# Squares of the input weights computed on ScalarE instead of VectorE, in front of the first correction row

## The chip, the cores and the metric

The kernel runs on the 8 cores of one Trainium2 chip. Each core computes 2048 of the 16384 tokens with the same program; no core waits for another. The metric is the device time in microseconds (us) of the slowest core. The engines of a core are named as in the profile: PE (TensorE, matmuls), PEld (its weight loads), DVE (VectorE), ACT (ScalarE), POOL (GpSimd) and SP (SyncE); POOL and SP issue the DMAs here.

## The reference

Positive random features replace attention, then a gated feed-forward layer; both with a residual and a layer norm.

```
def _rfs(xw, ab, AB, gs):
    dot_products = einsum('...d,rd->...r', xw, ab[:, None] * gs)
    correction = (0.5 * sum(xw * xw, axis=-1))[..., None] * (ab * ab)
    return 1.0 / sqrt(NUM_RFS) * AB * exp(dot_products - correction)

ab = xis;  AB = exp(xis)
weights = _rfs(input_weights, ab, AB, proj_matrix)     # [1024, 1024]
feats   = _rfs(x, ab, AB, proj_matrix)                 # [16384, 1024]
x = layernorm(x + einsum('bsr,or->bso', feats, weights))
gate = x @ (w_gate/127).T;  up = x @ (w_up/127).T      # 1024 -> 3072
x = layernorm(x + (silu(gate) * up) @ (w_down/127).T)  # 3072 -> 1024
```

What the change touches is `sum(xw * xw)` for `xw = input_weights`: the squares of a 1024 x 1024 matrix, summed over its inner dimension.

## The kernel before

A core's tokens are worked in four tiles of 512. In the first half (features), tile by tile, `emit_mm1(t)` computes the projections of the tile on PE in eight groups (`rc`) of eight 128x512 matmuls (line 268) and one single-row matmul (line 273) that adds the correction; ACT turns each group into features by an exponential (line 281). `emit_mm2(t)` multiplies the features with `weights` (lines 410, 416 and 422) and layer norm follows. The second half is the feed-forward layer (lines 565, 603, 658 to 674).

The order on every engine is the order in which the program is written: `Sched` keeps one list for each engine, `wait` puts a wait for a semaphore's value into it, and `inc` an instruction that raises one. ACT and DVE also wait for their own instruction before, through their own semaphore. No scheduler moves anything, so what stands behind a wait in a list waits too.

The start goes as follows.

- POOL issues all loads one behind the other (line 169): `xfm` of tile 0, the row `xisr`, two halves of `projT`, then `iwT` (the input weights, 8192 columns on 128 partitions), `xfm` of tile 1 and later `wgT`. `iwT` has a semaphore of its own, `Liw`.
- `emit_xsq(0)`: DVE squares tile 0 of x into the buffer XSQ (line 200). `emit_ones_mm(0)`: PE sums the squares with a column of ones (line 235, tile `pt3`). `emit_srow(0)`: ACT scales the sum and writes the row that the correction matmuls read (line 249).
- `emit_mm1(0)` waits for that row, with `em.wait("tensor", "SE", ev["se_srow", t])`, and runs its eight groups.
- `emit_iwsq(dk)`, for dk 0 to 7: DVE squares one eighth of `iwT` (128x1024, line 213) into one of two halves of XSQ. `emit_swones(dk)`: PE sums it with two 1x512 matmuls (line 289), accumulating over dk in PSUM. DVE waits before square dk for the sums of dk - 2, since the halves alternate.
- `emit_swrow()`: ACT makes the correction row of the weights (line 301). `emit_dotw()`: PE projects the input weights, eight groups of sixteen 128x512 matmuls (line 313) and two single-row ones (line 320), and ACT writes `weights` by an exponential (line 332).
- `emit_xsq(1)`: DVE squares tile 1 of x into XSQ, once the last sum of the weights' squares has been read from it.

X1TB is a buffer of 8192 columns that is first written by the evacuation of transposed layer-norm outputs in tile 1 (line 456), and by an SP load of `x1s` into its second half behind that.

Of the kernel before, what the change touches and what calls it, by code (L numbers as in the profile page):

```python
# [14 lines left out]
AF = mybir.ActivationFunctionType  # L15
OP = mybir.AluOpType
# [7 lines left out]
DK = D // 128  # L24
# [11 lines left out]
X1TB_O = X1TOK_O + 4096  # L36
PROJT_O = X1TB_O + 8192
IWT_O = PROJT_O + 8192
WT_O = IWT_O + 8192
XFM_O = WT_O + 8192  # L40
XSQ_O = XFM_O + 8192
# [52 lines left out]
def build_nc(stage=3, lnlv=5):  # L94
# [13 lines left out]
    with ExitStack() as stack:  # L108
        e = stack.enter_context
# [13 lines left out]
        em = Sched(sems)  # L123
        ev = {}

        def bf(a, b):
            return BF[:, a:a + b]

        def bfr(a, b):
            return BF[0:1, a:a + b]  # L130
# [8 lines left out]
        ones_col = bf(ONES_O, 1)  # L139
# [31 lines left out]
        def xfsem(t):  # L171
            return "Lxf" + str(t % 2)
# [20 lines left out]
        def emit_xsq(t):  # L193
            em.wait("vector", xfsem(t), ev["ld_xfm", t])
            if t >= 1:
                em.wait("vector", "MM", ev.get(("mm_swones", DK - 1)) if t == 1 else ev["mm_ones", t - 1])
            for h in range(2):
                ev["gs_xsq", t, h] = em.inc(
                    "vector", "VE",
                    lambda e, t=t, h=h: e.tensor_tensor(  # L200
                        bf(XSQ_O + h * 2048, 2048),
                        bf(XFM_O + (t % 2) * 4096 + h * 2048, 2048),
                        bf(XFM_O + (t % 2) * 4096 + h * 2048, 2048), OP.mult))

        def emit_iwsq(dk):
            em.wait("vector", "Liw", ev["ld_iwT"])
            if dk == 0:
                em.wait("vector", "MM", ev["mm_ones", 0])
            if dk >= 2:
                em.wait("vector", "MM", ev["mm_swones", dk - 2])  # L210
            ev["gs_iwsq", dk] = em.inc(
                "vector", "VE",
                lambda e, dk=dk: e.tensor_tensor(  # L213
                    bf(XSQ_O + (dk % 2) * 1024, 1024), bf(IWT_O + dk * 1024, 1024),
                    bf(IWT_O + dk * 1024, 1024), OP.mult))

        ftmp = fa(FTMP_O, DK)
        em.wait("vector", "XR", XR_ALL)
# [8 lines left out]
        def emit_ones_mm(t):  # L227
            em.wait("tensor", "VE", ev["ve_consts"])
            if t >= 1:
                em.wait("tensor", "SE", ev["se_srow", t - 1])  # L230
            for dk in range(DK):
                if dk % 4 == 0:
                    em.wait("tensor", "VE", ev["gs_xsq", t, dk // 4])
                def f(e, dk=dk, t=t):
                    return e.matmul(prow[:, :], ones_col,  # L235
                                    bf(XSQ_O + dk * 512, 512),
                                    start=(dk == 0), stop=(dk == DK - 1))
                if dk == DK - 1:
                    ev["mm_ones", t] = em.inc("tensor", "MM", f)
                else:  # L240
                    em.raw("tensor", lambda e, f=f: f(e))

        def emit_srow(t):
            em.wait("scalar", "MM", ev["mm_ones", t])
            if t >= 2:
                em.wait("scalar", "MM", ev["mm_dot", 8 * (t - 2) + RC - 1])
            ev["se_srow", t] = em.inc(
                "scalar", "SE",
                lambda e, t=t: e.activation(  # L249
                    bfr(SROW_O + (t % 2) * 512, 512), prow[:, :], AF.Identity,  # L250
                    bias=c512[0:1, :], scale=-0.5))
# [31 lines left out]
                        bias=biasF[:, rc:rc + 1], scale=xisc[:, rc:rc + 1]))  # L283

        def emit_swones(dk):
            em.wait("tensor", "VE", ev["gs_iwsq", dk])
            for oh in range(2):
                def f(e, dk=dk, oh=oh):
                    return e.matmul(P1[0:1, 1024 + oh * 512:1024 + oh * 512 + 512],
                                    ones_col, bf(XSQ_O + (dk % 2) * 1024 + oh * 512, 512),  # L290
                                    start=(dk == 0), stop=(dk == DK - 1))
                if oh == 1:
                    ev["mm_swones", dk] = em.inc("tensor", "MM", f)
                else:
                    em.raw("tensor", lambda e, f=f: f(e))
# [139 lines left out]
        def emit_tr(t, m):  # L435
            i = 4 * t + m
            em.wait("tensor", "SE", ev["se_apply", i])
            if i >= 1:
                em.wait("tensor", "VE", ev["ve_evac", i - 1])
            for dk in range(DK):  # L440
                def f(e, dk=dk, i=i):
                    return e.transpose(ptr[:, dk * 128:dk * 128 + 128],  # L442
                                       bf(X1TOK_O + (i % 4) * 1024 + dk * 128, 128),
                                       ident)
                if dk == DK - 1:
                    ev["mm_tr", i] = em.inc("tensor", "MM", f)
                else:
                    em.raw("tensor", lambda e, f=f: f(e))
            em.wait("vector", "MM", ev["mm_tr", i])
            if m == 0:  # L450
                em.wait("vector", "XSS", 16 * t)
            dst = BF[:, X1TB_O:X1TB_O + 4096].rearrange(
                "p (dk t) -> p dk t", dk=DK)[:, :, m * 128:m * 128 + 128]
            srcp = ptr[:, :].rearrange("p (dk t) -> p dk t", dk=DK)
            ev["ve_evac", i] = em.inc(
                "vector", "VE", lambda e, dst=dst, srcp=srcp: e.tensor_copy(dst, srcp))
            if m == 3:
                em.wait("sync", "VE", ev["ve_evac", i])
                em.wait("sync", "XSS", 16 * t)
                ev["xs_st", t] = em.inc(  # L460
                    "sync", "XSS",
                    lambda e, t=t: e.dma_start(
                        x1s_h[:, t * 4096:(t + 1) * 4096], bf(X1TB_O, 4096)), 16)
                if t == 0:
                    em.wait("sync", "XSS", ev["xs_st", 0])
                    ev["xs_ld", 0] = em.inc(
                        "sync", "XSL",
                        lambda e: e.dma_start(bf(X1TB_O + 4096, 4096),
                                              x1s_h[:, 0:4096]), 16)

        emit_xsq(0)
        emit_ones_mm(0)
        emit_srow(0)
        emit_mm1(0)
        for dk in range(DK):
            emit_iwsq(dk)
            emit_swones(dk)
        emit_swrow()
        emit_dotw()
        ev["ld_wgT"] = dma("gpsimd", "Lwg", bf(WGT_O, 24576), wgT_h[:, :])  # L480
        emit_xsq(1)
        emit_ones_mm(1)
        emit_srow(1)
# [136 lines left out]
        for pi, t in enumerate(B_ORDER):  # L620
# [26 lines left out]
            for m in range(4):  # L647
                i = 4 * pi + m
# [72 lines left out]
def _get_nc():  # L721
    global _NC_CACHE
    if _NC_CACHE is None:
        _NC_CACHE = build_nc()
    return _NC_CACHE
# [42 lines left out]
```

How the kernel before makes its waits and increments, by code:

```python
    def wait(self, eng, sem, val):  # L74
        if val is None or val <= 0:
            return
        assert val <= self.c[sem], f"wait on future event {sem}={val} > {self.c[sem]}"
        key = (eng, sem)
        if self.lastwait.get(key, 0) >= val:
            return
        self.lastwait[key] = val
        h = self.sems[sem]
        self.q[eng].append(lambda e, h=h, v=val: e.wait_ge(h, v))
# [1 line left out]
    def inc(self, eng, sem, fn, n=1):  # L85
        if (eng in ("vector", "scalar")) or (eng == "gpsimd" and sem == "GS"):
            self.wait(eng, sem, self.c[sem])
        h = self.sems[sem]
        self.c[sem] += n
        self.q[eng].append(lambda e, fn=fn, h=h, n=n: fn(e).then_inc(h, n))
        return self.c[sem]
# [2 lines left out]
def build_nc(stage=3, lnlv=5):  # L94
# [56 lines left out]
            if hc < 8:  # L151
                base = XSQ_O + hc * 512
            elif hc < 16:
                base = FEATS_O + (hc - 8) * 512
            elif hc < 20:
                base = IWT_O + 6144 + (hc - 16) * 512
            else:
                base = X1TOK_O + (hc - 20) * 512
            return bf(base + lo, n)
        em.raw("sync", lambda e: e.dma_start(fa(FXISC_O, DK), xisc_h[:, :]).then_inc(sems["XR"], 16))
        em.c["XR"] += 16
        XR_ALL = em.c["XR"]
```

## Time and profile before

| | us |
|---|---|
| median of 3 runs | 738.04 |
| lowest and highest of them | 737.9, 738.67 |
| the profiled execution's own time | 738.42 |
| its span on the slowest core (core 1) | 736.9 |
| spans of the eight cores | 733.8 to 736.9 |
| PE busy on core 1 | 702.6 (95% of the span) |
| DVE busy, ACT busy | 182.6, 197.0 |

All rows come from one profiled execution, and where nothing else is said, from core 1. Times count from the first instruction of that core. A timeline row merges instructions of one line that follow each other (xcount), gives the start and the length in us, and in brackets how long the engine had been idle before and what released it. The clock (PEclk) is the share of full TensorE speed that the chip granted.

### The profile page before, as it was taken

What the parts mean: (1) busy time and instruction counts of PE and PEld (TensorE: products, weight loads), DVE (VectorE), ACT (ScalarE), POOL (GpSimd) and SP (SyncE); (2) the same over time, 40 slices, a digit from 0 to 9 for tenths busy, and PEclk for the clock granted to TensorE, in tenths of its full rate; (3) what the DMA queues carried; (4) which work ended last, traced back from release to release, by engine and by line L of the source; (5) the groups of instructions that cost most, each with busy time, mean ns of one, the idle gap of its engine ahead of it and who ended that gap; (6) DMA issues with size and microseconds to landing.
All of it is one profiled execution on the core that took longest, in us unless ns stands there. A gap on an engine that the chain in (4) does not pass through costs nothing.

```text
span 736.9 us, 9045 instructions; the slowest of 8 cores (733.8 to 736.9 us)
## 1 busy us (share of the span) xinstructions
PE 702.6 (95%) x3424; PEld 314.2 (43%) x3424; DVE 182.6 (25%) x327; ACT 197.0 (27%) x322; POOL 8.0 (1%) x19
## 2 busy tenths in 40 slices
PE   1989999999979999999999999999999999999994
PEld 0323444444444444444444444444444444444442
DVE  1040143444352111122221121221212131211222
ACT  0312235353551111043311105231110523111122
POOL 2000000000000000000000000000000000000000
PEclk9999999999989999999999999999999999999997
DMA  8990030591057000001200000120000100000011
GB/s 124 167 367 28 1 58 1 121 390 60 1 225 289 1 1 1 1 28 58 87 0 1 1 1 29 58 86 0 1 0 3 57 29 29 0 1 2 1 58 57
DMA packets 5547, 44.63 MB, mean 61 GB/s; under 512 B 768, under 2 KB 768, under 8 KB 2816
## 3 DMA queue, kind: packets, MB, share of 16 engines
q0 software_dynamic: 1904, 27.27, 13.4%
q1 hardware_dynamic: 3600, 16.78, 6.1%
q8 instruction: 28, 0.46, 0.3%
q14 instruction: 15, 0.12, 0.1%
HBM read 30.42 MB, written 12.58 MB: 58 GB/s over the span
## 4 chain that ended last, share of the span: by engine, by line
PE 90%; DMA 5%; DVE 2%; ACT 1%; issue 1%; POOL 0%; DVEq 0%; ACTq 0%; POOLq 0%
PE pt L603 23%; PE P L565 22%; PE P L658 22%; PE P L410 6%; PE P L268 6%; DMA bfarena<-iwT 5%; PE P L313 4%; PE P L273 1%; PE P L664 1%; PE P L674 1%; PE P L416 1%; PE P L422 1%; PE pt L442 1%; PE pt L235 1%; DVE bfarena L213 1%
## 5 line engine op out<-in xcount | busy, mean ns | idle before, releaser
L565 PE MATMUL P<-bfarena 128*128 128x512 bf16 x768 | 184.6, 382 | 0.4 <-ACT bfarena L584 0.4
L603 PE MATMUL pt<-bfarena 128*128 128x512 bf16 x768 | 181.8, 379 | 0.0
L658 PE MATMUL P<-bfarena 128*128 128x512 bf16 x736 | 163.2, 379 | 0.0
L616 DVE SCALAR_TENSOR_TENSOR bfarena<-pt,bfarena 128x512 bf16<-128x512 f32 x96 | 66.4, 692 | 245.5 <-PE pt L603 236.8
L584 ACT ACTIVATE bfarena<-P 128x512 bf16<-128x512 f32 x96 | 57.3, 597 | 237.2 <-PE P L565 229.1
L565 PEld LDWEIGHTS P<-bfarena 128*128 128x128 bf16 x768 | 75.1, 98 | 93.2 <-issue 2.5
L603 PEld LDWEIGHTS pt<-bfarena 128*128 128x128 bf16 x768 | 74.9, 97 | 92.5
L658 PEld LDWEIGHTS P<-bfarena 128*128 128x128 bf16 x736 | 71.9, 98 | 88.7
L357 DVE TENSOR_SCALAR_CACHE_REDUCE bfarena<-P 128x1024 bf16<-128x1024 f32 x32 | 39.2, 1225 | 202.6 <-PE P L674 144.9
L268 PE MATMUL P<-bfarena 128*128 128x512 bf16 x256 | 62.9, 388 | 2.3 <-ACT bfarena L249 2.3
L377 ACT ACTIVATE f32arena<-f32arena 128x1 f32<-128x1 f32 x32 | 9.4, 295 | 176.5 <-DVE f32arena L374 175.6
L410 PE MATMUL P<-bfarena 128*128 128x512 bf16 x224 | 51.5, 379 | 0.0
L281 ACT ACTIVATE bfarena<-P,f32arena 128x512 bf16<-128x512 f32 x32 | 24.9, 778 | 57.1 <-PE P L273 57.1
L268 PEld LDWEIGHTS P<-bfarena 128*128 128x128 bf16 x256 | 23.0, 99 | 34.3 <-issue 11.2
L313 PE MATMUL P<-bfarena 128*128 128x512 bf16 x128 | 31.0, 396 | 1.4 <-ACT bfarena L301 1.4
L410 PEld LDWEIGHTS P<-bfarena 128*128 128x128 bf16 x224 | 21.3, 98 | 24.3 <-issue 0.4
L235 PE MATMUL pt<-bfarena 128*1 128x512 bf16 x32 | 9.4, 440 | 13.6 <-DVE bfarena L200 13.5
L313 PEld LDWEIGHTS P<-bfarena 128*128 128x128 bf16 x128 | 12.3, 101 | 19.6 <-issue 7.1
L388 ACT ACTIVATE bfarena<-bfarena,f32arena 128x1024 bf16<-128x1024 bf16 x16 | 19.8, 1240 | 1.5
L388 ACT ACTIVATE f32arena<-bfarena,f32arena 128x1024 f32<-128x1024 bf16 x16 | 19.8, 1240 | 1.5
L367 DVE SCALAR_TENSOR_TENSOR f32arena<-bfarena 128x1024 f32<-128x1024 bf16 x16 | 19.6, 1225 | 2.0 <-DVE f32arena L359 0.5
L367 DVE SCALAR_TENSOR_TENSOR bfarena<-bfarena 128x1024 bf16<-128x1024 bf16 x16 | 19.6, 1225 | 1.7
(53 smaller groups left out, 225.3 us busy)
## 6 DMA issues: line engine op xcount, KB each, us to landing
out<-f32arena SPq DMA_DIRECT2D x16, 512.0 KB, 2.6
bfarena<-wgT POOLq DMA_DIRECT2D x1, 6144.0 KB, 54.2
bfarena<-wdT POOLq DMA_DIRECT2D x3, 2048.0 KB, 14.5
bfarena<-wuT POOLq DMA_DIRECT2D x1, 4608.0 KB, 26.9
bfarena<-xfm POOLq DMA_DIRECT2D x4, 1024.0 KB, 12.6
x1s<-bfarena SPq DMA_DIRECT2D x4, 1024.0 KB, 4.8
bfarena<-x1s SPq DMA_DIRECT2D x4, 1024.0 KB, 7.2
bfarena<-projT POOLq DMA_DIRECT2D x2, 1024.0 KB, 19.5
```

The lines of the kernel that those rows point to most:

```text
L268: em.raw("tensor", lambda e, rc=rc, dk=dk, xb=xb, ps=pslice: e.matmul(ps, pjap(rc, dk), bf(xb + dk * 512, 512), start=(dk == 0), stop=False))
L281: lambda e, rc=rc, ps=pslice: e.activation(bf(FEATS_O + rc * 512, 512), ps, AF.Exp, bias=biasF[:, rc:rc + 1], scale=xisc[:, rc:rc + 1]))
L313: em.raw("tensor", lambda e, rc=rc, dk=dk, oh=oh, base=base: e.matmul(P1[:, base + oh * 512:base + oh * 512 + 512], pjap(rc, dk), bf(IWT_O ...
L357: e.tensor_scalar(dv, ps, 1.0, 0.0, OP.mult, OP.add, accum_out=negS))
L367: e.scalar_tensor_tensor(out_ap, dv, 1.0, dv, OP.mult, OP.mult, accum_out=s2))
L388: lambda e, dv=dv, out_ap=out_ap, rc_=rc_, nmrs=nmrs: e.activation(out_ap, dv, AF.Identity, scale=rc_[:, 0:1], bias=nmrs))
L410: em.raw("tensor", lambda e, rc=rc, oh=oh, m=m, base=base: e.matmul(P1[:, base + oh * 512:base + oh * 512 + 512], bf(FEATS_O + rc * 512 + ...
L565: return e.matmul(pg, bf(WGT_O + dk * 3072 + hc * 128, 128), bf(xb1 + dk * 512, 512), start=(dk == 0), stop=(dk == DK - 1))
L584: "scalar", "SE", lambda e, j=j, pg=pg: e.activation(sg_ap(j), pg, AF.Silu, scale=1.0 / 127.0))
L603: return e.matmul(puj, bf(wu_off + hc * 128, 128), bf(xb1 + dk * 512, 512), start=(dk == 0), stop=(dk == DK - 1))
L616: "vector", "VE", lambda e, j=j, hc=hc, puj=puj: e.scalar_tensor_tensor(hact_ap(hc, 0, 512), puj, 1.0 / 16129.0, sg_ap(j), OP.mult, OP.mult))
L658: e.matmul(P1[:, base + oh * 512:base + oh * 512 + 512], hact_ap(hc, m * 128, 128), bf(reg + (hc % 8) * 1024 + oh * 512, 512), start=(hc = ...
```

## The change

The squares of the input weights go from DVE (`tensor_tensor` with OP.mult, into the two halves of XSQ) to ACT (`activation` with AF.Square, into the eight eighths of X1TB, one for each dk). ACT's squares wait for `Liw`, as DVE's did. In the written order six of them stand between `emit_ones_mm(0)` and `emit_srow(0)`, two behind `emit_srow(0)`, and all of them ahead of `emit_mm1(0)`. The sums wait for ACT's semaphore instead of DVE's. Three waits on the last sum follow from the new buffer: DVE before the first evacuation into X1TB, SP before the load into its second half, while `emit_xsq(1)` now waits for `mm_ones, 0` alone.

```diff
         def emit_xsq(t):
             em.wait("vector", xfsem(t), ev["ld_xfm", t])
             if t >= 1:
-                em.wait("vector", "MM", ev.get(("mm_swones", DK - 1)) if t == 1 else ev["mm_ones", t - 1])
+                em.wait("vector", "MM", ev["mm_ones", t - 1])
...
         def emit_iwsq(dk):
-            em.wait("vector", "Liw", ev["ld_iwT"])
-            if dk == 0:
-                em.wait("vector", "MM", ev["mm_ones", 0])
-            if dk >= 2:
-                em.wait("vector", "MM", ev["mm_swones", dk - 2])
-            ev["gs_iwsq", dk] = em.inc(
-                "vector", "VE",
-                lambda e, dk=dk: e.tensor_tensor(
-                    bf(XSQ_O + (dk % 2) * 1024, 1024), bf(IWT_O + dk * 1024, 1024),
-                    bf(IWT_O + dk * 1024, 1024), OP.mult))
+            em.wait("scalar", "Liw", ev["ld_iwT"])
+            ev["se_iwsq", dk] = em.inc(
+                "scalar", "SE",
+                lambda e, dk=dk: e.activation(
+                    bf(X1TB_O + dk * 1024, 1024),
+                    bf(IWT_O + dk * 1024, 1024), AF.Square))
...
         def emit_swones(dk):
-            em.wait("tensor", "VE", ev["gs_iwsq", dk])
+            em.wait("tensor", "SE", ev["se_iwsq", dk])
             for oh in range(2):
                 def f(e, dk=dk, oh=oh):
                     return e.matmul(P1[0:1, 1024 + oh * 512:1024 + oh * 512 + 512],
-                                    ones_col, bf(XSQ_O + (dk % 2) * 1024 + oh * 512, 512),
+                                    ones_col,
+                                    bf(X1TB_O + dk * 1024 + oh * 512, 512),
                                     start=(dk == 0), stop=(dk == DK - 1))
...
             em.wait("vector", "MM", ev["mm_tr", i])
+            if i == 0:
+                em.wait("vector", "MM", ev["mm_swones", DK - 1])
...
                 if t == 0:
+                    em.wait("sync", "MM", ev["mm_swones", DK - 1])
                     em.wait("sync", "XSS", ev["xs_st", 0])
...
         emit_xsq(0)
         emit_ones_mm(0)
+        for dk in range(6):
+            emit_iwsq(dk)
         emit_srow(0)
+        emit_iwsq(6)
+        emit_iwsq(7)
         emit_mm1(0)
         for dk in range(DK):
-            emit_iwsq(dk)
             emit_swones(dk)
         emit_swrow()
         emit_dotw()
```

ACT's list at its start, before. Line 249 makes the correction row of tile 0, 281 the features, 301 the correction row of the weights; MM counts PE's instructions, SE ACT's own.

```order
L249 ACTIVATE bfarena<-pt,f32arena 1x512 [waits MM]
L281 ACTIVATE bfarena<-P,f32arena 128x512 [waits MM,SE] x8
L301 ACTIVATE bfarena<-P 1x1024 [waits MM,SE]
L332 ACTIVATE bfarena<-P,f32arena 128x1024 [waits MM,VE,SE]
L332 ACTIVATE bfarena<-P,f32arena 128x1024 [waits MM,SE] x7
L249 ACTIVATE bfarena<-pt,f32arena 1x512 [waits MM,SE]
```

And after, where line 209 is the new square and the lines 245, 277, 298 and 329 are those that were 249, 281, 301 and 332.

```order
L209 ACTIVATE bfarena<-bfarena 128x1024 [waits Liw]
L209 ACTIVATE bfarena<-bfarena 128x1024 [waits SE] x5
L245 ACTIVATE bfarena<-pt,f32arena 1x512 [waits MM,SE]
L209 ACTIVATE bfarena<-bfarena 128x1024 [waits SE] x2
L277 ACTIVATE bfarena<-P,f32arena 128x512 [waits MM,SE] x8
L298 ACTIVATE bfarena<-P 1x1024 [waits MM,SE]
L329 ACTIVATE bfarena<-P,f32arena 128x1024 [waits MM,VE,SE]
L329 ACTIVATE bfarena<-P,f32arena 128x1024 [waits MM,SE] x7
```

The instruction that waits for `Liw` is now the first of ACT's list, with the correction row of tile 0 behind it in seventh place.

PE's list at the end of `emit_mm1(0)`, before: the last group of the features, then the sums of the weights' squares (line 289), each pair with its wait for DVE (VE); five of the eight pairs are left out here.

```order
L268 MATMUL P<-bfarena 128x512 x7
L273 MATMUL P<-bfarena 128x512
L289 MATMUL P<-bfarena 1x512 [waits VE]
L289 MATMUL P<-bfarena 1x512
L289 MATMUL P<-bfarena 1x512 [waits VE]
L289 MATMUL P<-bfarena 1x512
L289 MATMUL P<-bfarena 1x512 [waits VE]
L289 MATMUL P<-bfarena 1x512
```

And after, where line 285 is the sum and line 310 the first matmul of `emit_dotw()`.

```order
L264 MATMUL P<-bfarena 128x512 x7
L269 MATMUL P<-bfarena 128x512
L285 MATMUL P<-bfarena 1x512 x16
L310 MATMUL P<-bfarena 128x512 [waits SE,Liw]
L310 MATMUL P<-bfarena 128x512 x15
```

The sixteen sums stand at the same place of PE's list, now with no wait among them. The wait for ACT's correction row ahead of `emit_mm1(0)` is where it was.

## Rows read from the trace of the kernel before

**Rows 1.** Spans and mean granted clock, three of the eight cores.

```profile
core 1: 736.9 us, clock 0.988
core 4: 736.5 us, clock 0.991
core 7: 735.3 us, clock 0.993
```

**Rows 2.** PE's waits, all of the span: total us, times, longest.

```profile
PE pt L235 <- DVE bfarena L200: 13.5, 1, 13.5
PE pt L442 <- DVE bfarena L456: 3.6, 2, 3.3
PE P L268 <- ACT bfarena L249: 2.3, 1, 2.3
PE P L289 <- DVE bfarena L213: 2.0, 8, 0.6
PE P L313 <- ACT bfarena L301: 1.4, 1, 1.4
```

**Rows 3.** Chain that ended last, in order of time, the load of iwT.

```profile
3.77 34.16 DMA bfarena<-iwT
```

**Rows 4.** Timeline of core 1, from the first ACT instruction to the first features.

```profile
17.20 1.28 ACT L249 ACT_TABLE_LOAD   x1 [17.20 <-PE pt L235]
18.50 0.68 ACT L249 ACTIVATE bfarena<-pt,f32arena 1x512 bf16<-1x512 f32 x1
...
19.43 3.52 PE L268 MATMUL P<-bfarena 128*128 128x512 bf16 x8 [2.31 <-ACT bfarena L249]
...
23.42 0.78 ACT L281 ACTIVATE bfarena<-P,f32arena 128x512 bf16<-128x512 f32 x1 [4.25 <-PE P L273]
...
25.59 0.78 ACT L281 ACTIVATE bfarena<-P,f32arena 128x512 bf16<-128x512 f32 x1 [1.39 <-PE P L273]
```

**Rows 5.** Timeline of core 1, from the end of emit_mm1(0) to emit_dotw().

```profile
38.05 0.39 PE L273 MATMUL P<-bfarena 1*128 1x512 bf16 x1
38.16 6.32 DVE L213 TENSOR_TENSOR bfarena<-bfarena 128x1024 bf16<-128x1024 bf16 x8 [23.43 <-DMA bfarena<-iwT]
...
39.00 0.59 PE L289 MATMUL P<-bfarena 128*1 128x512 bf16 x2 [0.56 <-DVE bfarena L213]
...
44.63 0.59 PE L289 MATMUL P<-bfarena 128*1 128x512 bf16 x2 [0.21 <-DVE bfarena L213]
45.37 1.01 ACT L301 ACTIVATE bfarena<-P 1x1024 bf16<-1x1024 f32 x1 [6.00 <-PE P L289]
...
46.64 5.31 PE L313 MATMUL P<-bfarena 128*128 128x512 bf16 x16 [1.42 <-ACT bfarena L301]
...
81.34 1.91 PE L235 MATMUL pt<-bfarena 128*1 128x512 bf16 x8
```

**Rows 6.** ACT's instructions grouped by line and form: count, busy us, mean ns.

```profile
L584 ACT ACTIVATE bfarena<-P 128x512 bf16<-128x512 f32 x96 | 57.3, 597 | 237.2 <-PE P L565 229.1 <-DVE bfarena L616 7.6
L281 ACT ACTIVATE bfarena<-P,f32arena 128x512 bf16<-128x512 f32 x32 | 24.9, 778 | 57.1 <-PE P L273 57.1
L388 ACT ACTIVATE bfarena<-bfarena,f32arena 128x1024 bf16<-128x1024 bf16 x16 | 19.8, 1240 | 1.5
L332 ACT ACTIVATE bfarena<-P,f32arena 128x1024 bf16<-128x1024 f32 x8 | 9.6, 1204 | 26.7 <-PE P L320 26.7
L301 ACT ACTIVATE bfarena<-P 1x1024 bf16<-1x1024 f32 x1 | 1.0, 1014 | 6.0 <-PE P L289 6.0
```

**Rows 7.** Timeline of core 1, two ACT instructions of a layer norm in a row.

```profile
91.81 0.30 ACT L384 ACTIVATE f32arena<-f32arena 128x1 f32<-128x1 f32 x1
92.19 1.24 ACT L388 ACTIVATE bfarena<-bfarena,f32arena 128x1024 bf16<-128x1024 bf16 x1
```

**Rows 8.** PE by stretch on core 1: us, busy (x), PEclk, DMA share, GB/s.

```profile
45.30:46.60 1.30, 0.00 (x0) 1.00 1.06 454
46.60:52.00 5.40, 5.36 (x17) 0.68 0.97 413
```

**Rows 9.** Timeline of core 4, the first group of emit_dotw().

```profile
46.35 3.65 PE L313 MATMUL P<-bfarena 128*128 128x512 bf16 x15 [1.42 <-ACT bfarena L301]
49.93 0.60 PE L320 MATMUL P<-bfarena 1*128 1x512 bf16 x2
```

**Rows 10.** Timeline of core 7, the correction row and the second group's features.

```profile
18.30 0.68 ACT L249 ACTIVATE bfarena<-pt,f32arena 1x512 bf16<-1x512 f32 x1
...
26.53 0.78 ACT L281 ACTIVATE bfarena<-P,f32arena 128x512 bf16<-128x512 f32 x1 [2.26 <-PE P L273]
```

## The prediction, made before the changed kernel had run

> **What bounds the kernel now.** I read four views, in this order. The cores first: core 1 ends last, core 4 0.4 us before it and core 7 1.6 us before it, and the program is the same on all, so one core's timeline can be followed as long as the spread is kept in mind [rows 1]. Then PE's waits, since PE is busy for 95% of the span. They are few: 13.5 us at the start for the first tile of x, 2.3 us for ACT's first correction row, 2.0 us in eight pieces for DVE's squares of the input weights, 1.4 us for the weights' correction row, and 3.6 us much later, for an evacuation [rows 2]. The edits touch the second, third and fourth. Third, the chain that ended last: it doesn't go through the features of tile 0 but through the load of iwT, issued at 3.77 and landing 34.16 us later, at 37.93 [rows 3]. So PE's work up to 38.4 lies beside a transfer, and nearly fills that time. Last, the timeline of the start, from which all terms come [rows 4, 5].
>
> In it the reader is to see two things. The features of tile 0 run from 19.43 to 38.44 and need nothing of iwT: what released them was the correction row on ACT, 18.50 to 19.18 [rows 4]. And DVE starts its squares at 38.16, 0.23 us behind the landing, while PE ends the features at 38.44: two things that end together [rows 5]. From 46.64 on PE runs almost without a pause, so a delay of that moment is a delay of the end.
>
> **The change part by part.** I follow core 1 to the start of the weights' projection (line 313), which is at 46.64 before. Nothing in the change touches the loads, so iwT still lands at 37.93.
>
> 1. *The wait for iwT moves ahead of the features.* ACT's list now begins with the square that waits for Liw. Behind it stand, on the same engine, five more squares and then the correction row of tile 0, and for that row waits all of PE's emit_mm1(0). DVE saw the landing 0.23 us later [rows 3, 5]; I give ACT the same, 38.16. Its first instruction carried the table load behind its wait: load at 17.20, 1.28 long, next instruction at 18.50 [rows 4]. So the first square starts at 38.16 + 1.30 = 39.46.
>
> 2. *Six squares.* The trace has no Square. The nearest is a 128x1024 SBUF to SBUF ACTIVATE with scale and bias read from memory, 1.240 us. Against the same from PSUM, 1.204, SBUF costs 0.036. The operands read from memory cost 0.18: 778 ns with them, 597 ns without, both 128x512. A 1x1024 one without them took 1.014. All of it in [rows 6]. So 1.240 - 0.18 = 1.06, or 1.014 + 0.036 = 1.05; I take 1.05, since the square reads no such operand, and keep 1.01 and 1.24 as bounds. Between two dependent ACT instructions lie 0.09 us (0.30 from 91.81 ends at 92.11, the next starts at 92.19) [rows 7]. Six squares: 5 x 1.14 + 1.05 = 6.75, ended at 46.21; bounds 6.5 and 7.9.
>
> 3. *The correction row and the features.* The row starts at 46.30, takes 0.68, ends at 46.98. PE came 0.25 later before (19.18 to 19.43) [rows 4], so the features start at 47.23 instead of 19.43: **27.80 us later**. They take the same 19.0 us. This includes their slow start: the first eight matmuls took 3.52 us where eight of the same length took 1.91 at full clock [rows 4, 5], which is the lower level, 1.2 GHz, after PE had idled. PE idles before this start in both kernels, for 2.3 us then and for about 30 now, and I take the same cost. Squares 6 and 7 take 2 x 1.14 = 2.3 us on ACT behind the row; the first features are due 4.25 us behind it [rows 4], so they are covered. Without that cover, if a square took over 2.1 us, the exponentials would come late.
>
> 4. *The sums lose their waits.* Before, the first sum started at 39.00, or 0.56 us of waiting behind the features, and the last ended at 45.22. After, all eight squares lie ready when the features end (near 66). Sixteen 1x512 matmuls at full clock: eight take 1.91 at line 235 [rows 5], so the distance is (1.91 - 0.38) / 7 = 0.22 and sixteen take 15 x 0.22 + 0.38 = 3.63. From 39.00 to 45.22 were 6.22: **2.6 us gained**, and **0.6 us** for the wait ahead of them. The bound on the other side is no gain, if the sums ran at the lower level: 16 x 0.44 = 7.0.
>
> 5. *The weights' correction row* keeps its 1.42 us of idle PE [rows 5]; it is what is late next when DVE's waits go.
>
> 6. *The clock of the weights' projection.* On core 1 the granted clock was 1.00 in 45.3 to 46.6 and 0.68 in the 5.4 us behind it (the lower level for most of a first group) [rows 8]: the first sixteen matmuls took 5.31. On core 4, behind the same 1.42 us of idle time, fifteen took 3.65 and the group's end came at 49.93 + 0.60, so 4.18 us after its start, against 5.85 us on core 1: the cost is 1.67 [rows 5, 8, 9]. Ahead of it PE had been fed in pairs with a pause each, on both. In the changed kernel it is fed without pauses, so I take the full clock on core 1, a gain of 1.67 there and of nothing on core 4. Both outcomes stay in the range.
>
> 7. *The rest costs nothing.* emit_xsq(1) no longer waits for the sums: off the path, since its reader stands behind the weights' projection. The two new waits for the last sum, on DVE before the first evacuation and on SP before the load into X1TB, ask for an event that is some 50 us old there (queued behind: the layer-norm work on DVE, stores of x1s on SP). DVE loses 8 squares, of which nothing waits.
>
> Two rules of the Trainium skill bear on this; nothing above depends on them. ScalarE: Activation LUTs, "Rules for kernel authors", gives multiplication to VectorE and not to ScalarE, which speaks against this change; the trace has DVE's eight squares in 6.32 us, 0.79 apiece with the gap, and by step 2 ACT's would be 1.14, so by that rule alone eight of them would cost 2.8 us more, off the path here once they lie ahead of the sums. The same page, "What ACT_TABLE_LOAD costs", adds a drain of about 1.38 us to a load of 1.283; the load agrees with [rows 4], but the next instruction there starts 0.02 us behind it, so the sum goes without the drain, and with it would be an estimated 1.4 us higher.
>
> **The sum.** Core 1: +27.80 - 0.60 - 2.6 = +24.6, less 1.67 for the clock, +22.9, to a span of 759.8. Core 4: 736.5 + 24.6 = 761.1, since iwT's landing drops out (both the old and the new start of the projection count from it) and it had nothing to regain. The slowest core then ends at 761.1, +24.2 against 736.9. I add 0.3 us for the slow start of the features, which was mostly hidden beside the load and is now on every core's path: from the start of the correction row to the second group's features core 1 took 25.59 - 18.50 = 7.09 us and core 7 26.53 - 18.30 = 8.23 [rows 4, 10], so the slowest of eight can pay up to 1.1 more. The profiled execution, 738.42 with a span of 736.9, would be at 762.9; the median of the runs, 738.04, is 0.4 lower and gives **762.5 us**.
>
> **The rivals.**
> - *One table doesn't serve all.* If the square's table lacks Identity and Exp, another load of 1.28 us comes ahead of the correction row, on the path; the further two, around squares 6 and 7, make 2 x 1.28 + 2.3 = 4.9 us on ACT against 4.25 to the first features, and those are not asked for by PE until its third group. So +1.3: 763.8. For it: no row shows Square. Against it: Identity and Exp run on one load at the start [rows 4]. (Trainium skill, ScalarE: Activation LUTs, "Table sets": cheap functions are in every set, though square isn't named there.) Chance 0.08.
> - *The clock turns against it.* The features' start like core 7's on the slowest core (+0.8 over my 0.3), and the lower level at the projection on a core that had not paid it before (core 4, +1.67): 762.5 + 2.5 = 765.0. For it: core 1's fall [rows 8]. Chance 0.08.
> - *Not slower: iwT comes early.* The new start of the projection is the landing plus 33.3 us (71.2 - 37.93), the old one 46.64. The change decides for itself if iwT lands by 13.3; then the squares run beside DVE's first ones and the gain of steps 4 and 6 is left, 738.0 - 3.2 - 1.3 = 733.5. Against it: 34.16 us from issue to landing, behind four loads that nothing here moves [rows 3]. Chance 0.02.
> - *The program doesn't hold back the row*, if ACT ran the correction row ahead of its squares. ACT's order is its list's; nothing speaks for it. The time would be about 735. Chance 0.01.
>
> **How the numbers follow.** The forecast has 0.81. Its own bounds: squares of 1.01 and 1.24 give -0.2 and +1.1, the slow start -0.6 to +0.8, the projection's clock 0 to +1.67 on the slowest core, and the level of the three runs +0.6. Together 761.3 to 764.5; with most of the first two rivals, and somewhat more below for a slowest core that regains clock, the range is 760.9 to 765.3. About 0.2% is what a measurement of this kernel can tell from no change: the last two rivals hold 0.03, of which 0.01 is for a landing near 13 that leaves the time as it was; so faster 0.02, same 0.01, slower 0.97.
>
> **What would show it.** Right: ACT idle until 38, then a table load, six squares of 1.05, and the first feature matmul near 47, with an idle time of about 30 us on PE put down to line 245; the sixteen sums in 3.6 us without waits; the projection starting near 71. A second table load would show the first rival, a clock under 1.00 behind 71 the second. Wrong would be a first feature matmul before 30, or PE pauses behind 71 that shrank by several us.

## The result and the profile after

The changed kernel takes 763.68 us (median of 8 runs, 763.16 to 764.56); the kernel before took 738.66 beside it. The ratio is 1.0341, 95% interval 1.0329 to 1.0353: 25.0 us slower. The forecast was 762.5, within 760.9 to 765.3. A time here is the median of all runs of a kernel; a ratio and its interval leave out the few runs in which the cores of a die had a lower granted clock and took several per cent longer.

The profiled execution took 763.16 us, the span of its slowest core, core 3, 761.6. Three cores of the list of spans, as in [rows 1]:

```profile
core 1: 758.7 us, clock 0.994
core 3: 761.6 us, clock 0.973
core 4: 760.9 us, clock 0.973
```

PE's waits on core 3, the view of [rows 2] (total us, times, longest). The 2.3 us ahead of the features have become 30.0, and DVE's pauses in the sums are gone. The wait at line 568, between the two halves of the kernel, is 0.4 us on core 1 of the kernel before (line 565 there) and differs from core to core; it comes up again below.

```profile
PE P L264 <- ACT bfarena L245: 30.0, 1, 30.0
PE pt L231 <- DVE bfarena L200: 13.5, 1, 13.5
PE pt L439 <- DVE bfarena L455: 3.3, 1, 3.3
PE P L568 <- ACT bfarena L587: 3.1, 1, 3.1
PE P L310 <- ACT bfarena L298: 1.4, 1, 1.4
```

The chain that ended last, in order of time, has the same load as [rows 3], landing at 37.82:

```profile
3.76 34.06 DMA bfarena<-iwT
```

And the timeline of core 3, to be laid beside [rows 4, 5]. Line 209 is the square, 245 the correction row of tile 0, 264 the features, 285 the sums, 298 the correction row of the weights, 310 the weights' projection.

```profile
37.89 1.28 ACT L209 ACT_TABLE_LOAD   x1 [37.89 <-DMA bfarena<-iwT]
39.19 6.80 ACT L209 ACTIVATE bfarena<-bfarena 128x1024 bf16<-128x1024 bf16 x6
...
46.08 0.68 ACT L245 ACTIVATE bfarena<-pt,f32arena 1x512 bf16<-1x512 f32 x1
46.85 2.21 ACT L209 ACTIVATE bfarena<-bfarena 128x1024 bf16<-128x1024 bf16 x2
...
47.01 3.57 PE L264 MATMUL P<-bfarena 128*128 128x512 bf16 x8 [29.98 <-ACT bfarena L245]
...
66.62 3.65 PE L285 MATMUL P<-bfarena 128*1 128x512 bf16 x16
...
70.42 1.01 ACT L298 ACTIVATE bfarena<-P 1x1024 bf16<-1x1024 f32 x1 [2.80 <-PE P L285]
...
71.69 3.65 PE L310 MATMUL P<-bfarena 128*128 128x512 bf16 x16 [1.42 <-ACT bfarena L298]
```

ACT is idle until iwT lands, then one table load, six squares, the row; PE's features begin 0.25 us behind the row, at 47.01 (19.43 before), and the projection at 71.69 (46.64 before). So the start is 25.05 us later than on core 1 before, and from there to the end it is 689.9 us on this core against 690.3 on that one.

One core says little of the others, so here are the stages in the mean of the eight cores of a profiled execution, in us. `wait_only` and `squares_behind` are two of the experiments below.

| | before | changed | wait_only | squares_behind |
|---|---|---|---|---|
| iwT lands at | 37.4 | 37.1 | 37.6 | 37.5 |
| features start at | 19.0 | 46.3 | 39.9 | 19.3 |
| from there to the first sum | 19.6 | 19.8 | 19.3 | 21.8 |
| from there to the projection | 7.6 | 5.1 | 5.1 | 10.4 |
| from there to the first feature product | 35.3 | 34.9 | 34.9 | 36.7 |
| from there to the end | 654.1 | 654.4 | 654.9 | 653.9 |
| span | 735.5 | 760.4 | 754.1 | 742.0 |

The features start 27.3 us later, the sums give back 2.6, and everything else is within 0.5. Between the landing of iwT and the first feature matmul lie 9.18 us, on every one of the eight cores, though the landing itself varies from 36.3 to 38.1.

### The profile page after: what moved, and what is told of

Its sections match the earlier page's. It is cut to its first block, busy times and chain, and to the rows that moved or that the text cites. A ratio compares the mean times of both kernels' runs of the same rounds, so it can differ in the third digit from the quotient of the medians.

```text
span 761.6 us, 9031 instructions; the slowest of 8 cores (758.7 to 761.6 us)
## 1 busy us (share of the span) xinstructions
PE 699.2 (92%) x3424; PEld 313.4 (41%) x3424; DVE 177.0 (23%) x319; ACT 205.7 (27%) x330; POOL 8.0 (1%) x19
## 4 chain that ended last, share of the span: by engine, by line
PE 91%; DMA 4%; ACT 2%; issue 1%; DVE 1%; POOL 0%; ACTq 0%; DVEq 0%; POOLq 0%
PE pt L606 22%; PE P L568 22%; PE P L661 21%; PE P L264 8%; PE P L407 6%; DMA bfarena<-iwT 4%; PE P L310 4%; PE P L269 1%; PE P L667 1%; PE P L413 1%; PE P L419 1%; PE P L677 1%; PE pt L439 1%; ACT bfarena L209 1%; PE pt L231 1%
## 5 line engine op out<-in xcount | busy, mean ns | idle before, releaser
L568 PEld LDWEIGHTS P<-bfarena 128*128 128x128 bf16 x768 | 74.9, 98 | 95.9 <-issue 5.4
L661 PEld LDWEIGHTS P<-bfarena 128*128 128x128 bf16 x736 | 71.9, 98 | 88.6
L264 PEld LDWEIGHTS P<-bfarena 128*128 128x128 bf16 x256 | 23.1, 99 | 62.5 <-issue 39.6
L407 PEld LDWEIGHTS P<-bfarena 128*128 128x128 bf16 x224 | 21.4, 98 | 24.3 <-issue 0.4
L200 DVE TENSOR_TENSOR bfarena<-bfarena 128x2048 bf16<-128x2048 bf16 x8 | 9.8, 1226 | 56.3 <-DMA bfarena<-xfm 55.9
L364 DVE SCALAR_TENSOR_TENSOR f32arena<-bfarena 128x1024 f32<-128x1024 bf16 x16 | 19.6, 1225 | 1.9 <-DVE f32arena L356 0.4
L364 DVE SCALAR_TENSOR_TENSOR bfarena<-bfarena 128x1024 bf16<-128x1024 bf16 x16 | 19.6, 1225 | 1.7
```

Source lines behind the costliest of these rows:

```text
L264: em.raw("tensor", lambda e, rc=rc, dk=dk, xb=xb, ps=pslice: e.matmul(ps, pjap(rc, dk), bf(xb + dk * 512, 512), start=(dk == 0), stop=False))
L364: e.scalar_tensor_tensor(out_ap, dv, 1.0, dv, OP.mult, OP.mult, accum_out=s2))
L407: em.raw("tensor", lambda e, rc=rc, oh=oh, m=m, base=base: e.matmul(P1[:, base + oh * 512:base + oh * 512 + 512], bf(FEATS_O + rc * 512 + ...
L568: return e.matmul(pg, bf(WGT_O + dk * 3072 + hc * 128, 128), bf(xb1 + dk * 512, 512), start=(dk == 0), stop=(dk == DK - 1))
L661: e.matmul(P1[:, base + oh * 512:base + oh * 512 + 512], hact_ap(hc, m * 128, 128), bf(reg + (hc % 8) * 1024 + oh * 512, 512), start=(hc = ...
```

## Experiments

The theory: PE's features need ScalarE, and ScalarE now stands in front of a transfer; the cost is the landing of iwT plus what is queued ahead of the first ScalarE result that PE asks for. The rivals: the squares are dear because they run on ScalarE; or only the correction row's place matters. A second question came from the trace: how much of it is TensorE's clock. Each kernel was timed beside the kernel before (738.63, 738.17 and 738.65 us in the three sets). Except for the last two they are small edits of the changed kernel or of the kernel before; where VectorE does the squares, the waits that follow from the eight places in X1TB are those of the changed kernel.

### The correction row ahead of all squares (row_first)

```diff
         emit_ones_mm(0)
-        for dk in range(6):
-            emit_iwsq(dk)
         emit_srow(0)
-        emit_iwsq(6)
-        emit_iwsq(7)
+        for dk in range(8):
+            emit_iwsq(dk)
         emit_mm1(0)
```

> Theory (whatever PE needs of ScalarE for the features stalls behind the squares that wait for iwT): with the correction row ahead of all eight squares PE runs two feature groups at once and then needs the first exponential, which stands behind the squares. Squares from landing + 0.2, 8 x 1.14 = 9.1, exponential 0.78, so PE resumes at landing + 10.4 instead of landing + 9.3, with six groups left instead of eight (2 x 2.17 = 4.3 less): 3.2 us faster than the changed kernel, about 760.5. Rival (only the row's seventh place costs): the time comes back to about 739. Rival (the cost is the amount of work on ScalarE): no difference, 763.7.

Measured: 760.2 us, ratio 1.0291 (1.0260 to 1.0322). That is 3.5 us under the changed kernel, where 3.2 were expected. Both rivals fall. The timeline of core 0 shows the wait in its new place:

```profile
24.46 0.38 PE L269 MATMUL P<-bfarena 1*128 1x512 bf16 x1
37.81 9.10 ACT L209 ACTIVATE bfarena<-bfarena 128x1024 bf16<-128x1024 bf16 x8 [19.18 <-DMA bfarena<-iwT]
...
47.00 1.65 ACT L277 ACTIVATE bfarena<-P,f32arena 128x512 bf16<-128x512 f32 x2
47.92 3.21 PE L264 MATMUL P<-bfarena 128*128 128x512 bf16 x8 [23.08 <-ACT bfarena L277]
```

PE does two groups, fills both halves of its PSUM tile and then waits 23.08 us for the first exponential (line 277), which stands behind all eight squares. The row is released and the stall only moves one ScalarE instruction further.

### Only the wait, with the squares on VectorE (wait_only)

The squares run on VectorE into X1TB, in their old place; what is left of the change's order is one wait.

```diff
         emit_ones_mm(0)
+        em.wait("scalar", "Liw", ev["ld_iwT"])
         emit_srow(0)
         emit_mm1(0)
         for dk in range(DK):
             emit_iwsq(dk)
             emit_swones(dk)
```

> Squares on VectorE, into the eight eighths of X1TB, in their old place; only the wait for iwT stands on ScalarE ahead of the correction row. Theory: row ends at landing + 0.2 + 1.3 + 0.7, so the features start 6.9 us earlier than in the changed kernel, and all behind is equal: 756.8. The wait alone is then 18 of the 25 us. Rival (the squares on ScalarE are the cost): about 739 to 741.

Measured: 757.98 us, ratio 1.0266 (1.0240 to 1.0292), 1.2 us over the expectation and inside its interval. A kernel with this wait and not one square on ScalarE is 19.4 us slower, of the 25. (The sums gain their 2.6 us here too, so the wait by itself costs more.) The timeline of core 7:

```profile
38.25 1.28 ACT L245 ACT_TABLE_LOAD   x1 [38.25 <-DMA bfarena<-iwT]
...
39.55 0.68 ACT L245 ACTIVATE bfarena<-pt,f32arena 1x512 bf16<-1x512 f32 x1
40.47 3.57 PE L264 MATMUL P<-bfarena 128*128 128x512 bf16 x8 [23.33 <-ACT bfarena L245]
```

From the start of the table load to the end of the row are 1.98 us here and 8.87 us in the changed kernel (37.89 to 46.76): the six squares and the pauses between them are the other 6.9 us. On every core the first feature matmul comes 2.35 us behind the landing of iwT here, and 9.18 in the changed kernel. By the times the difference is 5.7 us; in the profiled executions it is 6.3 in the mean of the cores, where iwT landed 0.5 us later in this kernel.

### The squares on ScalarE, behind the features (squares_behind)

```diff
         emit_ones_mm(0)
-        for dk in range(6):
-            emit_iwsq(dk)
         emit_srow(0)
-        emit_iwsq(6)
-        emit_iwsq(7)
         emit_mm1(0)
+        for dk in range(8):
+            emit_iwsq(dk)
         for dk in range(DK):
             emit_swones(dk)
```

> All eight squares on ScalarE, but behind the features' exponentials. Theory: the first square starts behind the last exponential, near 39.5, the last ends near 48.5, the sums follow one by one, the weights' projection starts near 50.7 instead of 46.6: +4.1 us on the kernel before, 742.8, up to 1.7 more on a core whose clock falls there. Rival (ScalarE is the wrong engine and that is what the change costs): most of the 25 us stays, 755 or more. The engine's rate alone, 8 x (1.14 - 0.79) = 2.8, would give 741.5.

Measured: 744.34 us, ratio 1.0086 (1.0062 to 1.0110). Same instructions on the same engines as in the changed kernel, 19 us less. What is left is 5.7 us, and 6.5 in the mean span of the profiled execution. There the projection starts 5.3 us later instead of the 4.1 expected: 4.6 between the end of the features and the projection, 0.4 for slower features, 0.3 because the features started later. The projection then takes 1.4 us longer in the mean. Its eight groups ran at full clock on core 4 alone (34.88 us from its start to the first line 407) and took 36.6 to 37.7 us on the other seven. On core 1 they had taken 36.54 before, so for that core the clock adds only 0.1. Timeline and PE by stretch (us, busy, count for each engine, then clock, DMA share, GB/s) of core 1:

```profile
41.18 9.09 ACT L209 ACTIVATE bfarena<-bfarena 128x1024 bf16<-128x1024 bf16 x8
...
43.53 7.90 PE L285 MATMUL P<-bfarena 128*1 128x512 bf16 x14 [0.55 <-ACT bfarena L209]
...
52.84 5.44 PE L310 MATMUL P<-bfarena 128*128 128x512 bf16 x16 [1.42 <-ACT bfarena L298]
```

```profile
39.00:50.00 11.00, 7.54 (x19) 1.08 (x17) 2.45 (x2) 8.96 (x9) 0.00 (x0) 0.68 1.06 358
50.00:52.00 2.00, 1.29 (x3) 0.11 (x2) 0.00 (x0) 0.69 (x2) 0.00 (x0) 0.50 1.06 451
```

PE had been idle for 2.22 us ahead of the first sum, and was then fed one pair of sums every 1.14 us:

```profile
42.38 0.59 PE L285 MATMUL P<-bfarena 128*1 128x512 bf16 x2 [2.22 <-ACT bfarena L209]
```

That pair ran at full clock. From the second to the fourth pair on, depending on the core, the matmuls of all eight cores are at the 1.2 GHz level, which is well ahead of the 1.42 us pause; core 4 alone was back at full clock when the projection began. Whether the 2.22 us pause or the thin feed behind it brought the fall, this kernel doesn't separate.

### Only the eight places (dve_eight)

The kernel before, with VectorE's squares written into X1TB and no other edit of the order. The diff leaves out the place from which the sums read, and the other waits that follow from the buffer.

```diff
-                em.wait("vector", "MM", ev["mm_swones", dk - 2])
...
-                    bf(XSQ_O + (dk % 2) * 1024, 1024), bf(IWT_O + dk * 1024, 1024),
+                    bf(X1TB_O + dk * 1024, 1024), bf(IWT_O + dk * 1024, 1024),
```

> The kernel before with one part of the change: the squares stay on VectorE in their old place, but go into eight places in X1TB instead of two halves of XSQ. Theory (the buffer was no bound on most cores, VectorE's pace is): the same as before within 0.2%, 738.5. Rival (the eight places are worth the 2.6 us that the sums gained in the changed kernel): 736.

Measured: 738.44 us, ratio 0.9999 (0.9990 to 1.0008). The buffer is free and brings nothing in the time: the sums go at VectorE's pace of 0.8 us for a square. From the first sum to the projection it took 7.0 to 7.6 us, against 7.64 before and 5.07 in the changed kernel.

### The load of iwT later (iw_load_later)

```diff
-        ev["ld_iwT"] = dma("gpsimd", "Liw", bf(IWT_O, 8192), iwT_h[:, :])
         ev["ld_xfm", 1] = dma("gpsimd", xfsem(1), xfm_dst(1), xfm_src(1))
+        ev["ld_iwT"] = dma("gpsimd", "Liw", bf(IWT_O, 8192), iwT_h[:, :])
```

> The changed kernel with the loads of iwT and of tile 1 of x issued in the other order. iwT then lands where tile 1 of x landed, near 44 instead of 37.5. Theory (the landing releases the whole start): every us of the landing is a us of the end, +6.2, 769.9. Rival (the features wait for something else): 763.7.

Measured: 770.95 us, ratio 1.0441 (1.0423 to 1.0459), so 7.3 us over the changed kernel (two runs only). ACT's first row on core 4:

```profile
44.22 1.28 ACT L209 ACT_TABLE_LOAD   x1 [44.22 <-DMA bfarena<-iwT]
```

In the mean of the eight cores the landing went from 37.1 to 43.7 us and the span from 760.4 to 767.0: both 6.6 us. The first feature matmul is 9.18 us behind the landing on every core, as in the changed kernel. What the time has beyond that is not the landing's: on core 4, the slowest, the part from the first line 407 to the end took 656.9 us, against 655.0 on core 3 of the changed kernel. The transfer is what the whole start hangs on.

### PE kept busy ahead of the features (pe_kept_busy, pe_busy_longer)

In the traces the eight feature groups (from their first matmul to the first sum) took 18.79 to 20.12 us in the changed kernel, 19.8 in the mean, though eight groups at full clock are 17.3. Two kernels put matmuls whose result nobody reads into PE's 30 us pause.

```diff
+        em.wait("tensor", xfsem(0), ev["ld_xfm", 0])
+        for n in range(118):
+            em.raw("tensor", lambda e, n=n: e.matmul(
+                P1[0:1, 0:512], ones_col, bf(XFM_O + (n % 8) * 512, 512),
+                start=True, stop=True))
         emit_mm1(0)
```

> The changed kernel with 118 extra 1x512 matmuls whose result nobody reads, on PE ahead of the features, to fill most of its 30 us pause. Theory: the features' slow start was on every core's path (18.8 to 20.1 us for the eight groups, against 8 x 2.17 = 17.4 at full clock), so they start at the full clock and the slowest core gains 2 to 2.6 us: 761.3. Rival (the slow start isn't on the path or isn't due to the pause): 763.7.

Measured: 763.5 us, ratio 1.0342 (1.0323 to 1.0360). Nothing gained in time. The features took 18.9 us in the mean, 0.9 less, but they also started 1.1 us later, mostly because iwT landed at 38.1 in the mean instead of 37.1. Whether the unread matmuls delay that transfer or whether it is chance, no run shows; the same was seen in the next two kernels (38.0 and 38.2), while the other kernels with the loads in the old order have 37.1 to 37.7. And the pause wasn't filled: on core 7 the fill ran out 3.85 us early, and the first eight matmuls took as long as in the changed kernel.

```profile
17.19 26.79 PE L480 MATMUL P<-bfarena 128*1 128x512 bf16 x118
47.83 3.57 PE L264 MATMUL P<-bfarena 128*128 128x512 bf16 x8 [3.85 <-ACT bfarena L245]
```

With 126 of them:

> As pe_kept_busy, with 126 unread matmuls instead of 118, so that PE's pause ahead of the features is near 2 us instead of 3.9, behind which the features still started at the lower clock. Theory (the slow start is the clock's and on the path): features take 17.4 to 17.6 us instead of 18.8 to 20.1, the slowest core gains 2 to 2.6 us, 761.3. Rival (the slow start comes in any case, or what it costs is given back behind): 763.6.

Measured: 764.44 us, ratio 1.0350 (1.0335 to 1.0365), another miss of the time. But now the cores differ within one run. Core 6 and core 1:

```profile
46.53 1.90 PE L264 MATMUL P<-bfarena 128*128 128x512 bf16 x8 [1.54 <-ACT bfarena L245]
```

```profile
47.52 3.22 PE L264 MATMUL P<-bfarena 128*128 128x512 bf16 x8 [2.86 <-ACT bfarena L245]
```

Behind a pause of 1.4 to 1.8 us the features ran at full clock (cores 3, 6 and 7: 17.32 us for the eight groups), behind 2.2 to 3.1 us mostly not (18.67 to 18.90 on cores 0, 1, 2 and 5; core 4, with 2.68, kept it). The mean over cores fell from 19.8 to 18.1 us. So the slow start is the clock's. That the time didn't follow has two reasons. iwT landed 0.9 us later in the mean (0.5 on core 1, the slowest, against core 3 of the changed kernel). And from the start of the first feature product (line 407) to the end, the cores took 653.4 to 656.6 us: core 1 had both 18.90 for its features and 656.6 here. Its two pauses between the halves of the kernel, from PE's waits and its stretches:

```profile
PE pt L439 <- DVE bfarena L455: 3.2, 1, 3.2
PE P L573 <- ACT bfarena L592: 3.1, 1, 3.1
```

```profile
240.00:244.00 4.00, 0.85 (x6) 0.81 1.03 428
244.00:248.00 4.00, 4.00 (x16) 0.50 1.05 438
```

### Both pauses filled (both_pauses_filled)

The changed kernel with 131 unread matmuls ahead of the features and 10 in each of the two pauses between the halves.

```diff
                 for hc in range(4):
+                    if hc == 1:
+                        emit_fill(10)
                     emit_tr(NT - 1, hc)
+                    if hc == 2:
+                        emit_fill(10)
                     emit_gate(pi, hc, mm_only=True)
```

> The changed kernel with 131 unread matmuls ahead of the features, and 10 each (into the idle row of pt3) in the two pauses of PE between the halves of the kernel, where the traces have 3.3 us and 0.2 to 3.1 us and a fall of the clock that differs from core to core (from the start of the first feature product to the end 653.4 to 656.6 us). Theory (the last filled kernels gained on the features, and the slowest core lost it again in those pauses): features 17.3 us on nearly all cores, 653.4 behind them on all, slowest span about 759, time 760.8, 2.9 us under the changed kernel. Rival (PE's clock is not what differs): 763.6.

Measured: 761.16 us, ratio 1.0299 (1.0283 to 1.0315), 2.5 us under the changed kernel by the medians and 3.1 by the ratios. From line 407 to the end all eight cores now took 653.4 to 653.9 us. The features took 17.1 to 17.3 on five cores, one of which had a pause of 2.5 us ahead of them, and 18.8 to 18.95 on the other three, whose pauses were 2.3 to 2.4. So a filled pause returns what the clock costs, in two places. Only the place ahead of the features belongs to the change's loss: from the first feature product to the end the kernel before varies as well, from 653.3 to 655.3 us. The pause itself, which is most of the loss, stays.

### Sums behind the first group of the projection (sums_behind, sums_behind_seam)

The kernel before has pauses of its own there: VectorE's pace in the sums and the wait for the weights' correction row. Neither is needed where it stands, since the row only enters a group at its last two matmuls. This kernel starts from dve_eight, puts the sums into pt3, and writes out the first two groups of the projection by hand (`dotw_main` is the loop over dk of `emit_dotw`, `dotw_end` the two correction matmuls and the exponential).

```diff
         emit_mm1(0)
+        em.wait("tensor", "Liw", ev["ld_iwT"])
+        dotw_main(0, range(DK))
         for dk in range(DK):
             emit_iwsq(dk)
             emit_swones(dk)
         emit_swrow()
-        emit_dotw()
+        dotw_main(1, range(4))
+        dotw_end(0)
+        dotw_main(1, range(4, DK))
+        dotw_end(1)
+        for rc in range(2, RC):
+            dotw_main(rc, range(DK))
+            dotw_end(rc)
```

> Squares on VectorE into X1TB, but the sums (into the tile pt3 instead of P) stand behind the first sixteen matmuls of the weights' projection, and the correction matmuls of the first group in the middle of the second group. Theory (in the kernel before PE lost time to VectorE's pace in the sums and to the 1.4 us of the correction row, and neither is needed there): PE goes on without a pause from 38.4, the 4.0 us of pauses go (8.2 us from the end of the features to the projection against 3.5 for the sums), and so does the clock's fall: 4.6 to 6 us faster than before, 733.5. Rival (something behind gives it back, a later load for example): 738.6.

Measured: 733.78 us, ratio 0.9935 (0.9923 to 0.9948), 4.8 us under the kernel before by the ratio (4.4 by the medians), while the changed kernel is 25 over it. The timeline of core 7, where line 309 is the projection, 287 the sums, 320 the correction matmuls:

```profile
38.30 3.65 PE L309 MATMUL P<-bfarena 128*128 128x512 bf16 x16 [0.18 <-DMA bfarena<-iwT]
38.32 6.28 DVE L209 TENSOR_TENSOR bfarena<-bfarena 128x1024 bf16<-128x1024 bf16 x8 [23.88 <-DMA bfarena<-iwT]
41.88 3.65 PE L287 MATMUL pt<-bfarena 128*1 128x512 bf16 x16
...
45.46 1.92 PE L309 MATMUL P<-bfarena 128*128 128x512 bf16 x8
45.68 1.01 ACT L300 ACTIVATE bfarena<-pt 1x1024 bf16<-1x1024 f32 x1 [6.63 <-PE pt L287]
47.31 0.60 PE L320 MATMUL P<-bfarena 1*128 1x512 bf16 x2
```

The sixteen sums take 3.65 us instead of 6.2, and both ACT's row and VectorE's squares lie beside PE's work. Adding the fills between the halves:

> sums_behind with the 10 and 10 unread matmuls in the two pauses between the halves. Theory: the span behind the first feature product is 653.4 on all cores instead of up to 655, so 1 to 1.5 us under sums_behind, 732.5. Rival (the fills come in the way, because a pause is shorter than 2.2 us): equal or slower, 733.8 to 735.

Measured: 733.42 us, ratio 0.9927 (0.9914 to 0.9940). The part from the first feature product to the end went from 653.6 to 655.6 us down to 653.7 to 654.1, as expected (653.4), but the time fell by only 0.4 us, where 1 to 1.5 were expected. That is within the intervals: not settled as a gain.

## Why the prediction was right, and where it was off

The forecast of 762.5 missed the measured 763.68 by 1.2 us, and the steps came in the order that it gave. Point by point, on core 3 (landing at 37.82) against the predicted core 1 (37.93).

1. *The wait moves ahead of the features*: as forecast, one table load of 1.28 us, first square at 39.19 (39.46). ScalarE saw the landing 0.07 us behind it, not 0.23. wait_only shows that the wait alone, without a square on ScalarE, gives 19.4 us, and iw_load_later shows that the end follows the landing.
2. *Six squares*: 6.80 us against 6.75. The group of eight has a mean of 1057 ns; the 1.05 taken from neighbours without operands from memory was right, the upper bound of 1.24 was far off.

```profile
L209 ACT ACTIVATE bfarena<-bfarena 128x1024 bf16<-128x1024 bf16 x8 | 8.5, 1057 | 0.7
```

3. *The row and the features*: features from 47.01 (47.23). Squares 6 and 7 took 2.21 us and were covered. Here is the term that was mis-sized: their length. Predicted was core 1's 19.0 and 0.3 more for the spread; the eight cores took 19.8 in the mean, and five of them 19.85 to 20.12. Before, two cores took as long (19.95 and 20.07), and most of it lay beside the load. So the term was 0.5 us short in the mean. It hardly shows in the end, since iwT landed 0.3 us earlier in the mean: the profiled execution took 763.16 us with a span of 761.6, where the prediction has 762.9 and 761.4. Of the 1.2 us between 762.5 and 763.68, 0.6 is that the runs of before were at 738.66 beside it, not 738.04.
4. *The sums*: 3.65 us without a wait, against 6.22, so 2.6 us gained as forecast. From the first sum to the projection it took 5.07 us on all cores, against 7.64 before. The wait ahead of the first sum is gone too; it was near 0.6 us on four cores before, as on core 1, and between 0 and 0.9 on the others.
5. *The weights' correction row*: 1.42 us of idle PE, unchanged.
6. *The clock of the projection*: full on all eight cores (34.87 us for its groups), against two cores at 36.54 before. The prediction's price for the fall rests on core 1's first group, 5.85 us long; its end is this row (51.89 + 0.60 - 46.64):

```profile
51.89 0.60 PE L320 MATMUL P<-bfarena 1*128 1x512 bf16 x2
```

The choice made in the prediction was right. squares_behind shows the other outcome, but there PE stood still for 2.2 us and was fed thinly behind that, and the clock was down before the 1.42 us pause began. That the dense sums are what kept the clock up in the changed kernel is likely, and not shown.
7. *The rest costs nothing*: none of the new waits shows up in PE's waits on core 3.

Two pieces of the prediction's arithmetic don't follow. Its own bounds, added up, give 761.7 to 766.7, not the 761.3 to 764.5 that it states; the measured time lies inside both. And the 1.3 us in the rival of the early landing has no source; step 6 has 1.67, on core 1 alone.

The two rules from the Trainium skill (ScalarE: Activation LUTs) can now be read against rows. Its rule for VectorE, "Rules for kernel authors", points the right way: off the critical wait, in squares_behind, ScalarE costs 5.7 us more than VectorE, its later start and the clock's fall included. But that is less than a quarter of the 25 us that the changed kernel lost. Its drain of 1.38 us behind a table load, in "What ACT_TABLE_LOAD costs", isn't seen: the load at 37.89 lasts 1.28 and the square starts at 39.19.

Of the rivals, a second table load didn't come: Square, Identity and Exp ran on the load at 37.89, and the next one on core 3 is at 241.54. Of the rival in which the clock turns, the half at the projection didn't come. The other half, a start of the features like core 7's, did come on most cores (first eight matmuls in 3.57 us on seven of eight), and it is the 0.5 us of step 3. The early landing, and a program in which the row isn't held back by the squares, are both refuted by the 30.0 us wait.

Open is what decides, at a given pause, whether the clock falls on a core: 2.68 us kept it on one core and lost it on another, and 2.5 kept it where 2.3 lost it. Open is also why iwT landed later in the three kernels with unread matmuls ahead of the features. That the second pause between the halves (line 568, or 573 with the fills) comes out anywhere from 0.2 to 3.8 us is read from traces; that the fills even out what follows was run, but the order of work that makes these pauses wasn't changed.

## What to carry to other kernels

An engine with an in-order list is blocked by the latest input of its first waiting instruction. Before a step is given to an idle engine, ask what the busiest engine will want from that engine while the step waits for its data; ScalarE was idle for the first 17 us here, but squares that need a transfer landing at 38 can't use that time. A term that is only needed at the end of an accumulation can be computed behind the accumulation's start: that gave 4.8 us where the move to ScalarE lost 25.

## What the runs showed of the hardware

The granted clock recorded for a stretch can read 1.00 while matmuls run at the lower level. The features of the kernel before started with eight 128x512 matmuls in 3.52 us, where 1.9 is full clock [rows 4]; PE on the same core in that stretch (us, busy, count, clock, DMA share, GB/s):

```profile
19.00:23.00 4.00, 3.57 (x9) 1.00 1.06 166
```

In the changed kernel core 3 started them as slowly (3.57 us), and there the record has it, in the stretch that ends with this start (busy times of PE, PEld, DVE, ACT and POOL ahead of the clock):

```profile
37.00:50.00 13.00, 2.99 (x8) 1.05 (x8) 2.45 (x2) 10.42 (x10) 0.00 (x0) 0.50 1.06 348
```

Core 7 of the same execution started its features just as slowly (3.57 us), and its record reads 1.00 in that stretch:

```profile
37.00:50.00 13.00, 2.70 (x7) 1.05 (x8) 2.45 (x2) 10.41 (x10) 0.00 (x0) 1.00 1.05 348
```

So the mean clocks of the two, 0.973 and 0.992, differ mostly by what was recorded for an idle PE, and not by time (761.6 and 761.0 us). The length of the first matmuls behind a pause is the better evidence.
